# Attention in a two-layer audio tower: how the softmax's inverse sums reach the layout of the mixed values, and where the first layer's turned expert input is kept

## What is computed

```python
h = _L0_tok_ref(x, conv_w, conv_b, ln_gamma, ln_beta)
h = h + _L0_attn_ref(_layernorm(h), Wq, Wk, Wv, Wo)
h = h + _L0_ffn_ref(_layernorm(h), router_w, ..., sw_gate, sw_up, sw_down)
h = h + _L1_attn_ref(_layernorm(h), w_qkv, w_out)
h = h + _L1_ffn_ref(_layernorm(h), gate_w, gate_b, w1, b1, w2, b2)
```

## Time and profile before

| | us |
|---|---|
| median of 3 runs | 1119.5 |
| lowest, highest | 1118.37, 1121.49 |
| profiled execution, span from first to last instruction | 1118.0 |
| PE busy in the span | 1073.2 |
| ACT busy in the span | 525.8 |
| DVE busy in the span | 488.1 |
| POOL busy in the span | 320.7 |

### The profile page before, as it was taken

One profiled execution on the slowest core, in us unless ns is written; L12 is line 12 of the kernel. 1 busy time (PEld: TensorE's weight loads), 2 busy tenths in 40 slices (PEclk: granted clock), 3 DMA queues, 4 the chain that ended last, 5 costly groups with the idle time before them and its releaser, 6 DMA issues.

```text
span 1118.0 us, 23799 instructions
## 1 busy us (share of the span) xinstructions
PE 1073.2 (96%) x7550; PEld 906.5 (81%) x7550; DVE 488.1 (44%) x2591; ACT 525.8 (47%) x1904; POOL 320.7 (29%) x317
## 2 busy tenths in 40 slices
PE   8999997999999999899998799999999999999996
PEld 7788876876666668677776699999999999999995
DVE  5779997622222323568988422222222222222221
ACT  2999999421112112999998033333323333332331
POOL 3222533413433442003226512222212222221222
PEclk9999999999999999999999899999999999999998
DMA  9932010156566644049101199999999998999980
GB/s 329 379 127 76 21 40 36 44 153 176 115 173 153 137 81 94 1 137 361 35 27 44 56 349 322 313 307 318 311 312 320 316 314 304 310 315 318 319 283 10
DMA packets 152006, 219.06 MB, mean 196 GB/s; under 512 B 15422, under 2 KB 124437, under 8 KB 151408
## 3 DMA queue, kind: packets, MB, share of 16 engines
q1 hardware_dynamic: 132976, 203.41, 53.2%
q0 software_dynamic: 18944, 14.62, 7.4%
HBM read 184.74 MB, written 43.09 MB: 204 GB/s over the span
## 4 chain that ended last, share of the span: by engine, by line
PE 79%; ACT 9%; DVE 3%; issue 3%; SPq 2%; DMA 2%; POOL 1%; POOLq 0%; DVEq 0%; ACTq 0%
PE bank L1075 21%; PE bank L1088 19%; PE bank L944 9%; PE bank L954 6%; ACT probs L1151 5%; PE bank L831 3%; PE bank L799 3%; PE bank L912 3%; PE bank L921 2%; PE bank L822 2%; PE bank L845 2%; PE bank L775 2%; PE bank L808 1%; PE bank L872 1%; PE bank L930 1%
## 5 line engine op out<-in xcount | busy, mean ns | idle before, releaser
L1318 ACT ACTIVATE dhidT<-bank,b1T 128x128 f32<-128x128 f32 x512 | 145.9, 368 | 308.9 <-PE bank L1075 308.9
L1075 PE MATMUL bank<-probsT,arena 128*128 128x128 f32 x2048 | 240.9, 277 | 0.1
L1075 PEld LDWEIGHTS bank<-probsT,arena 128*128 128x128 f32 x2048 | 235.5, 193 | 0.4 <-DVE probsT L1738 0.3
L1088 PE MATMUL bank<-arena,dhidT 128*128 128x256 f32 x1024 | 231.5, 380 | 0.0
L1088 PEld LDWEIGHTS bank<-arena,dhidT 128*128 128x128 f32 x1024 | 190.1, 191 | 22.9
L747 POOL DMA_INDIRECT out<-probsT,slot_token x64 | 98.6, 1540 | 375.5 <-DMA out<-probsT,slot_token 299.1
L1151 ACT ACTIVATE probs<-probs,neg_max 128x128 f32<-128x128 f32 x512 | 197.7, 393 | 1.6 <-DVE neg_max L1424 1.4
L1756 DVE TENSOR_TENSOR probsT<-bank,b_wide 128x256 f32<-128x256 f32 x64 | 27.2, 425 | 346.3 <-PE bank L1088 346.3
L1424 DVE CUSTOM_DVE_ANT_0 probs<-bank,mask 128x128 f32<-128x128 f32 x512 | 112.7, 284 | 11.6 <-PE bank L822 11.1
L718 POOL DMA_INDIRECT stream<-arena,slot_token x48 | 72.6, 1513 | 128.9 <-DVE arena L1618 94.7
L944 PE MATMUL bank<-rowsT,arena 128*128 128x320 f32 (+1 forms) x384 | 108.9, 436 | 0.2 <-DVE arena L1609 0.2
(11 more groups left out here) (162 smaller groups left out, 1368.7 us busy)
## 6 DMA issues: line engine op xcount, KB each, us to landing
arena<-L_ffn_w SPq DMA_DIRECT2D x128, 1024.0 KB, 7.3
rows<-zeros SPq DMA_DIRECT2D x13, 1024.0 KB, 12.1
drows<-rows SPq DMA_DIRECT2D x64, 132.0 KB, 7.5
arena<-L_ffn_w_gate SPq DMA_DIRECT2D x16, 352.0 KB, 4.4
arena<-L_ffn_w_up SPq DMA_DIRECT2D x16, 352.0 KB, 5.5
early<-rows SPq DMA_DIRECT2D x16, 264.0 KB, 3.5
early<-x SPq DMA_DIRECT2D x8, 512.0 KB, 6.8
arena<-L_ffn_w_down SPq DMA_DIRECT2D x16, 256.0 KB, 2.8
```

The costliest lines, as they stand in the source:

```text
L1075: mm = pe.matmul(bank[2 + 2 * (u % 2) + half][:, jj * P:(jj + 1) * P], w1_sb[u][:, c, j * P:(j + 1) * P], drowsT[:, u % 2, c, :], start=c ...
L1088: last_ = pe.matmul(bank[6 + u % 2][:, 0:D], dhidT[:, u % 2, j, :], w2_sb[u][:, j, :], start=j == 0, stop=j == J1 - 1)
L1318: last_ = act.activation(dhidT[:, u % 2, j, :], bank[2 + 2 * (u % 2) + half][:, jj * P:(jj + 1) * P], ACT.Gelu, bias=b1T[:, j, bass.ds(e, 1)])
```

## The change

1. `exp_inv` becomes 128 x 2 x 16 x 16. `invert` reads `exp_sum[:, t, :]` with each element repeated 16 times and writes the reciprocals 256 wide.
2. `turn_inverse` transposes four 128 x 128 blocks of it straight into the layout of `mix_bank`, in the place where `spread_inverse` stood. `spread_inverse`, `keep_inverse`, `exp_invT`, `own_rows` and the jobs SPREAD go; `keep_inverse` is now the name of the copy to `inv_rows`. 16 jobs fewer take part in the turn of the three banks.
3. In layer 0 `keep_ffn_inT` writes straight into `all_inT`, `route` and `shared_gate_up` both read there, and `keep_for_shared` goes with its semaphore.
4. The constants of `own_rows` and the zeroing of `exp_invT` go.

```diff
-        exp_inv = sb("exp_inv", [P, 2, HEADS])
-        own_rows = sb("own_rows", [P, D])
-        exp_invT = sb("exp_invT", [P, 2 * P])
+        exp_inv = sb("exp_inv", [P, 2, HEADS, HD])
...
+        def turned_input(L, i):
+            return all_inT[:, :, 2 * P * i:2 * P * (i + 1)] if L is L0 else ffn_inT[:, :, :]
...
             def turn_inverse(L, i):
                 pe.wait_ge(L.inv_done, 2 * i + 2)
                 bk, full = new_job(L, i, INVERSE)
-                for t in range(2):
-                    last = pe.transpose(bk[0:HEADS, t * P:(t + 1) * P], exp_inv[:, t, :], ident[:, :])
-                last.then_inc(full, 1)
-
-            def spread_inverse(L, i):
-                bk, full = new_job(L, i, SPREAD, (i, INVERSE))
-                for m in range(DC):
-                    last = pe.matmul(bk[:, m * D:(m + 1) * D], own_rows[:, m * P:(m + 1) * P], exp_invT[:, :],
-                                     start=True, stop=True)
+                wide = exp_inv[:, :, :, :].rearrange("p t h d -> p t (h d)")
+                for c in range(DC):
+                    for t in range(2):
+                        last = pe.transpose(bk[:, (2 * c + t) * P:(2 * c + t + 1) * P], wide[:, t, c * P:(c + 1) * P], ident[:, :])
                 last.then_inc(full, 1)
...
             def keep_inverse(L, i):
-                if L is L0 and i == 0:
-                    act.wait_ge(inv_zeroed, 1)
-                bk, free = from_job(L, i, INVERSE, (i - 1, SPREAD))
-                act.activation(exp_invT[0:HEADS, :], bk[0:HEADS, 0:2 * P], ACT.Copy).then_inc(free, 1)
-
-            def keep_spread(L, i):
                 wait(act, L.mix_done, i)
-                bk, free = from_job(L, i, SPREAD)
+                bk, free = from_job(L, i, INVERSE)
                 act.activation(inv_rows[:, :, :], bk[:, :].rearrange("p (c n) -> p c n", c=DC), ACT.Copy).then_inc(free, 1)
 
             def keep_ffn_inT(L, i):
-                if L is L0:
-                    wait(act, L0.input_kept, i)
-                bk, free = from_job(L, i, TURN_FFN, (i - 1, ROUTE))
-                act.activation(ffn_inT[:, :, :], bk[:, :].rearrange("p (c n) -> p c n", c=DC), ACT.Copy).then_inc(free, 1)
-
-            def keep_for_shared(i):
-                wait_read(act, L0, (i, TURN_FFN))
-                act.activation(all_inT[:, :, bass.ts(i, 2 * P)], ffn_inT[:, :, :], ACT.Copy).then_inc(L0.input_kept, 1)
+                bk, free = from_job(L, i, TURN_FFN, *(((i - 1, ROUTE),) if L is L1 else ()))
+                act.activation(turned_input(L, i), bk[:, :].rearrange("p (c n) -> p c n", c=DC), ACT.Copy).then_inc(free, 1)
...
             def invert(L, i, t):
                 dve.wait_ge(L.exp_done, 8 * i + 4 * t + 4)
                 wait_written(dve, L, (i - 1, INVERSE))
-                dve.reciprocal(exp_inv[:, t, :], exp_sum[:, t, :]).then_inc(L.inv_done, 1)
+                dve.reciprocal(exp_inv[:, t, :, :], over(exp_sum[:, t, :], 2, [P, HEADS, HD])).then_inc(L.inv_done, 1)
...
             def normalise(L, i):
...
-                wait_read(dve, L, (i, SPREAD))
+                wait_read(dve, L, (i, INVERSE))
```

More of the change, by code:

```diff
@@ L351, in build @@
         job_free = [sem(f"job_free{b}") for b in range(len(job_bank))]
-        CONV0, CONV1, TURN, Q, K, V, INVERSE, SPREAD, OUT, TURN_FFN, ROUTE, COUNT = range(12)
+        CONV0, CONV1, TURN, Q, K, V, INVERSE, OUT, TURN_FFN, ROUTE, COUNT = range(11)
         PROBS, GATE_UP, SHARED_DOWN, ROWS, DOWN = 12, 20, 23, 24, 26
@@ L1047, in _ @@
+            turn_probs(L1, 7, 1, 2); count(L1, 5); turn_inverse(L1, 7); turn_probs(L1, 7, 1, 3); turn_ffn_in(L1, 6)
             values(L1, 7, 1); route(L1, 6); project_out(L1, 7); count(L1, 6); keep_warm(14); turn_ffn_in(L1, 7); route(L1, 7); count(L1, 7); keep_warm(52)
@@ L1217, in _ @@
             keep_turned(L0, 0, 1, 1); keep_turned(L0, 0, 1, 2); exponentials(L0, 1, 0, 0); exponentials(L0, 1, 0, 1); keep_v(L0, 1)
-            keep_turned(L0, 1, 0, 0); keep_normedT(L0, 2); exponentials(L0, 1, 0, 2); keep_inverse(L0, 0); exponentials(L0, 1, 0, 3)
-            keep_k(L0, 2); keep_spread(L0, 0); keep_q(L0, 2); keep_turned(L0, 1, 0, 1); keep_turned(L0, 1, 0, 2)
+            keep_turned(L0, 1, 0, 0); keep_normedT(L0, 2); exponentials(L0, 1, 0, 2); exponentials(L0, 1, 0, 3)
+            keep_k(L0, 2); keep_inverse(L0, 0); keep_q(L0, 2); keep_turned(L0, 1, 0, 1); keep_turned(L0, 1, 0, 2)
             exponentials(L0, 1, 1, 0); exponentials(L0, 1, 1, 1); exponentials(L0, 1, 1, 2); exponentials(L0, 1, 1, 3)
@@ L1280, in _ @@
             keep_turned(L1, 2, 1, 0); keep_turned(L1, 2, 1, 1); keep_turned(L1, 2, 1, 2); exponentials(L1, 3, 0, 0)
-            exponentials(L1, 3, 0, 1); keep_normedT(L1, 4); keep_v(L1, 3); keep_inverse(L1, 2); exponentials(L1, 3, 0, 2)
-            keep_k(L1, 4); exponentials(L1, 3, 0, 3); keep_spread(L1, 2); keep_ffn_inT(L1, 1); keep_q(L1, 4)
+            exponentials(L1, 3, 0, 1); keep_normedT(L1, 4); keep_v(L1, 3); exponentials(L1, 3, 0, 2)
+            keep_k(L1, 4); exponentials(L1, 3, 0, 3); keep_inverse(L1, 2); keep_ffn_inT(L1, 1); keep_q(L1, 4)
             keep_turned(L1, 3, 0, 0); keep_turned(L1, 3, 0, 1); keep_turned(L1, 3, 0, 2); exponentials(L1, 3, 1, 0)
@@ L1285, in _ @@
             keep_turned(L1, 3, 1, 1); keep_turned(L1, 3, 1, 2); router_exp(L1, 1); exponentials(L1, 4, 0, 0)
-            exponentials(L1, 4, 0, 1); keep_normedT(L1, 5); keep_v(L1, 4); keep_inverse(L1, 3); exponentials(L1, 4, 0, 2)
-            exponentials(L1, 4, 0, 3); keep_spread(L1, 3); keep_q(L1, 5); keep_turned(L1, 4, 0, 0); keep_turned(L1, 4, 0, 1)
+            exponentials(L1, 4, 0, 1); keep_normedT(L1, 5); keep_v(L1, 4); exponentials(L1, 4, 0, 2)
+            exponentials(L1, 4, 0, 3); keep_inverse(L1, 3); keep_q(L1, 5); keep_turned(L1, 4, 0, 0); keep_turned(L1, 4, 0, 1)
             keep_turned(L1, 4, 0, 2); keep_ffn_inT(L1, 2); exponentials(L1, 4, 1, 0); exponentials(L1, 4, 1, 1); keep_k(L1, 5)
@@ L1337, in _ @@
             dve.memset(ones_b[:, :], 1.0)
-            dve.memset(exp_invT[:, :], 0.0).then_inc(inv_zeroed, 1)
-            dve.wait_ge(const_p, 19)
+            dve.wait_ge(const_p, 16)
             dve.tensor_scalar(row_id[:, 1:2], row_id[:, 0:1], HD.bit_length() - 1, 1, ALU.logical_shift_right,
```

168 lines of the change are left out of this document (78 added, 90 removed).

## The result

The changed kernel takes **1154.35 us** (median of 4 runs, 1152.22 to 1156.29), the kernel before beside it 1119.14 (4 runs, 1118.37 to 1121.49): ratio 1.0305, 95% interval 1.0286 to 1.0325. The forecast was 1140 us with a range of 1125 to 1157, and slower with a chance of 0.85. The direction and the engine were right, and the size was short by 14 us. The profiled execution has a span of 1150.9 us where it had 1118.0.

The account below looks back on a forecast made before the run. PE bounds layer 0's attention and ACT layer 1's, with DVE nearly full; VectorE becomes the bound. 8.1 + 3.0 + 6.4 + 2.8 = 20.3 us on 1118.0 gives 1138.3; the median stands 1.5 higher: 1140 us, range 1125 to 1157.

Parts of the forecast that it names:

- Which engine: Both attention middles: VectorE becomes the bound through the wide inversions, with greatest queued behind each; chance 0.70.
- The sign that VectorE would be over 95% busy: Changed kernel's profile, middles of both attention stages: DVE over 95% busy, with PE and ACT below 93%.
- The price: Each of 32 inversions on VectorE: 1640 ns for 256 elements at 5.8 ns each, 1.4 us more than now.
- The cheap price (the rival at 1112.5): VectorE's wide reciprocal costs only a copy's 0.42 us, so PE's and ACT's savings count: 1112.5 us; chance 0.10.
- the second rival: No change: a reciprocal costs 0.70 us on VectorE, 0.46 more, and the extra work fits: about 1119 us; chance 0.05.
- the slower rival: An element costs more than the slope says: 2.3 us for each VectorE inversion, 2.03 more, 1155 us; chance 0.15.
- A bounding engine does not lose such waits wholly; I let two thirds go.: Layer 0, 80 to 180 us: 14 us added, 5.9 of VectorE's 8.9 idle us taken up, +8.1 us.
- Layer 1's middle: Layer 1, 500 to 600 us: 14 us added, 7.6 of VectorE's 11.4 idle us taken up, +6.4 us.
- The ends: Outside the middles: 0 before 80 us, 0 after 180 us, +3.0 us from 445 to 500, +2.8 us at layer 1's end.
- Layer 1 up to the fifth inversion: Layer 1, 445 to 500 us: one inversion counted whole, three half, less about 0.5 for ACT's copies: +3.0 us.
- The last two inversions: End of layer 1: two inversions stand together, the last on the chain, and both count whole: +2.8 us.
- none of the idle time is taken up: Bound at the same price for both layers: 14 + 3 + 14 + 2.8 = 34 us, 1153 us.

Follow-up runs that it names:

- The dose runs: Kernel before with only the reciprocal widened, to 4 and 8 columns for each head (64 and 128 elements): 1122.45 us, ratio 1.0022, and 1129.05 us, ratio 1.0083.

## Why the prediction was right, and where its size was off

**Which engine.** Right. Ten inversions in each middle, each 1.5 us longer, made VectorE the engine that ends last in both, and `greatest` behind them is what the others wait for. The width alone, with all of TensorE's old work kept, reproduces the loss, so TensorE's saving was worth almost nothing. The sign that VectorE would be over 95% busy did not come (89.98 and 93.13), for the reason given below under the step that failed.

**The price.** Right to 6%: 1.64 us said, 1.744 measured. The dose runs show why the slope of two narrow rows, 5.8 ns for each element, was enough: from 16 to 64, 128 and 256 elements each one costs 6.2 ns ((546 - 247)/48, (946 - 546)/64, (1744 - 946)/128). The cheap price (the rival at 1112.5) and the second rival's 0.70 us are excluded, and the 2.3 us of the slower rival as well. The slower rival's *time* of 1155 was met, nearer than mine, but not by its mechanism. The Trainium skill, "VectorE: DVE Perf Modes", gives 0.96 GHz in its section "Specifications" and a repeat count of 8 in "First, the fixed hardware budget". Taken as eight cycles for each element, which the page does not say, they would be an estimate of 8.3 ns. The measurement decides: 6.2 ns, as long as six cycles of 0.96 GHz.

**"A bounding engine does not lose such waits wholly; I let two thirds go."** This step failed. I put 5.9 of the 8.9 idle us of layer 0's middle against the price, by analogy with PE and ACT, which run at 97 to 99% where they bound. The dose runs show that about 5 us of idle time stay between the fifth and the fourteenth inversion (6.5 before), whatever is added. In each of these traces some 3 us of it lie in about 80 gaps of under 0.2 us between VectorE's own instructions, and 1.3 us are one wait for GpSimd's `rstd`. Neither gets shorter when VectorE is late. What went is what VectorE had waited for TensorE. So its idle time was not mostly slack, and what PE and ACT reach where they bound says nothing of it. Between the fifth and the fourteenth inversion (83.65 and 170.52 us before, 84.87 and 186.03 after) nine prices, 13.5 us, became 14.3 us. 2.05 of these are the wait on the single buffer, so 1.2 us were taken up. I had +8.1 for ten prices.

**Layer 1's middle.** The same step failed here, more mildly. From the fifth inversion (507.55, then 527.28) to the first of the last two (605.60, then 634.99) ten prices, 15.0 us, gave 9.7: 5.3 were taken up, 7.6 predicted. ScalarE had bound here and VectorE really had time, 11.4 us in the 100 of the earlier trace rows, but it did not give two thirds of it.

**The ends.** Before 80 us: 0 said, 1.2 measured, so four inversions fitted. After 180 us: 0 said, 0.1 measured (15.5 late at the fourteenth inversion, 15.6 at the experts by their first weight load). Layer 1 up to the fifth inversion: +3.0 said, 3.5 measured (16.2 late to 19.7). The last two inversions: +2.8 said, 3.5 measured (29.4 late to 32.9). Between the first experts and layer 1's first inversion 0.6 more came in, and with it the parts add up to the 32.9 us of the two profiled executions. The method of reading what stands directly before and behind an inversion in the trace held where I used it.

**What I left out.** The wait on the single buffer, 2 us. The prediction counts what `turn_inverse` costs in its later place, but not the buffer that it frees.

**The bound.** Of the cases at my own price, "none of the idle time is taken up", 1153 us, came nearest. It was partly luck, as it had the price 0.1 too low, and neither the single buffer nor the part that was taken up in layer 1.

## What to carry to other kernels

Price a widened operation by the slope of its own rows, not by its count: one product saved on a full TensorE does not pay for 16 times the elements of a reciprocal on a VectorE at 91%. Idle time of an engine is not its reserve. See what it consists of: many short gaps between its own instructions and waits for an answer to what it has itself handed over stay when the engine becomes the bound. Two doses of work added to it, measured over the same work and not over a fixed window, show how much idle time stays. When a reader is moved later, look for the writer that waits for its buffer.

## What the runs showed of the hardware beside this

- A reciprocal on VectorE takes 147 ns and 6.2 ns for each element of a partition, over 16 to 256 elements. From 64 on, each sum was read 4, 8 or 16 times over by a broadcast.
- GpSimd's copy of 128x32 spread to 128x512 takes 0.61 us and ScalarE's 0.62, while VectorE's of 128x256 takes 0.29. GpSimd's products of 128x512 take 1.27.
- GpSimd's power takes 0.72 us for 128x2 and 5.44 for 128x32, 0.157 us for each element more.
- VectorE's idle time in layer 0's middle did not go below 5.0 us, with 0.30, 0.70 or 1.50 us added to each inversion.
- TensorE's mean granted clock from 80 to 180 us was 1.00 before and 0.95 in the changed kernel, with TensorE 97.11 and 86.74 us busy. With the width alone it was 87.90 us busy and the clock stayed at 1.00, and the first experts started at the same time.
